# Audio tower, one token layer with attention and a mixture of experts: expert weights split ahead of the first scatter, steps around the expert loop in another order, two groups' expert rows added by accumulating transfers

## The reference

```
h   = gelu(x[1:] @ W1 + x[0] @ W2 + b)                  # per sequence, 255 rows are left
h   = h + attention(layernorm(h))                       # 16 heads of 64, softmax over 255 keys
z   = layernorm(h)
p   = softmax(z @ router_w);  two best experts of 8 per row, with weights p
out = h + sum over the two experts of  p_e * (silu(z @ w1[e]) @ w2[e])
        + sigmoid(z @ gate_w) * ((silu(z @ gate) * (z @ up)) @ shared_down)
```

## Time and profile before

| | us |
|---|---|
| median of three executions | 1126.66 |
| lowest and highest | 1123.14, 1127.31 |
| the profiled execution | 1124.56 |
| its span (first to last recorded work) | 1122.8 |
| TensorE busy | 1054.9 |
| VectorE busy | 767.5 |
| ScalarE busy | 670.2 |
| GpSimd busy | 523.2 |

### The profile page before, as it was taken

The page is one execution under the profiler, slowest core; times in us unless marked ns, Lnnn a source line. Parts: engine busy times, 40 slices in busy tenths (PEclk is TensorE's granted clock), DMA queues, the critical chain, the costliest instruction groups (busy, mean ns, idle before and its releaser), DMA issues.

```text
span 1122.8 us, 23554 instructions
## 1 busy us (share of the span) xinstructions
PE 1054.9 (94%) x8042; PEld 882.3 (79%) x8042; DVE 767.5 (68%) x1975; ACT 670.2 (60%) x2059; POOL 523.2 (47%) x565
## 2 busy tenths in 40 slices
PE   6979999999999999999999999999998968899996
PEld 5867788878777887877788787878767868799985
DVE  3756766785777578577857867775774765466678
ACT  4647775774777477577747757774773534455541
POOL 0024543545546354654635464463444447544432
PEclk9989999999999999999999999999999999899998
DMA  8110000001000000100000010000022723344476
GB/s 262 58 44 1 2 1 20 2 3 38 20 1 30 30 1 1 39 20 1 30 22 9 1 40 20 2 30 16 15 68 84 236 75 112 102 141 134 125 303 212
DMA packets 46442, 65.93 MB, mean 59 GB/s; under 512 B 7960, under 2 KB 39448, under 8 KB 45304
## 3 DMA queue, kind: packets, MB, share of 16 engines
q1 hardware_dynamic: 39576, 46.60, 13.1%
q0 software_dynamic: 6480, 17.83, 4.3%
q10 hardware_dynamic: 272, 0.00, 0.0%
HBM read 36.09 MB, written 28.33 MB: 57 GB/s over the span
## 4 chain that ended last, share of the span: by engine, by line
PE 70%; DVE 9%; POOL 6%; issue 5%; ACT 2%; another core or an unknown queue 1%; DMA 1%; SPq 0%; DVEq 0%; ACTq 0%; POOLq 0%
PE pT_ps L710 10%; PE o_ps L723 9%; PE proj_ps L69 9%; PE proj_ps L71 9%; PE proj_ps L70 8%; PE s_ps L696 8%; POOL prob L1639 3%; PE v_ps L69 2%; POOL prob L1641 2%; PE v_ps L70 2%; PE v_ps L71 2%; PE s_ps L69 2%; PE s_ps L71 2%; PE s_ps L70 2%; PE pT_ps L955 2%
## 5 line engine op out<-in xcount | busy, mean ns | idle before, releaser
L1010 ACT ACTIVATE prob<-s_ps,nmax 128x255 f32<-128x255 f32 x512 | 239.0, 478 | 227.8 <-DVE nmax L1213 227.6
L1639 POOL TENSOR_SCALAR prob<-prob,rinv 128x255 f32<-128x255 f32 x128 | 139.7, 1091 | 373.5 <-DVE rinv L1231 370.6
L1213 DVE TENSOR_REDUCE nmax<-s_ps 128x2 f32<-128x510 f32 x256 | 166.3, 682 | 37.7 <-PE s_ps L696 36.2
L710 PEld LDWEIGHTS pT_ps<-ident,prob 128*128 128x128 f32 x1024 | 109.6, 141 | 60.8 <-issue 49.8
L710 PE MATMUL pT_ps<-ident,prob 128*128 128x128 f32 x1024 | 146.0, 281 | 6.7 <-POOL prob L1641 3.5
L1238 DVE COPY probT<-pT_ps 128x512 f32<-128x512 f32 x128 | 88.5, 691 | 77.0 <-PE pT_ps L710 77.0
L723 PE MATMUL o_ps<-probT,v 128*64 128x256 f32 x1024 | 139.6, 394 | 1.2 <-DVE oT_lo L1244 1.2
L696 PE MATMUL s_ps<-qk_space 64*128 64x256 f32 x1536 | 125.5, 296 | 5.3 <-ACT prob L1010 4.6
L1641 POOL TENSOR_SCALAR prob<-prob,rinv 128x255 f32<-128x255 f32 x128 | 119.2, 931 | 0.0
L696 PEld LDWEIGHTS s_ps<-qk_space 64*128 64x128 f32 x1536 | 99.2, 186 | 21.9 <-issue 8.7
L1010 ACT ACTIVATION_READ_ACCUMULATOR prob<-s_ps,nmax 128x1 f32 x512 | 106.3, 208 | 0.0
(11 more groups left out here) (268 smaller groups left out, 2739.4 us busy)
## 6 DMA issues: line engine op xcount, KB each, us to landing
xg<-expert_in_rows SPq DMA_DIRECT2D x71, 130.0 KB
back<-expert_out_rows SPq DMA_DIRECT2D x8, 1024.0 KB, 13.2
xin<-in_x_dram SPq DMA_DIRECT2D x8, 512.0 KB, 4.5
z_rows<-z SPq DMA_DIRECT2D x8, 512.0 KB, 3.2
z<-z_rows SPq DMA_DIRECT2D x8, 512.0 KB, 5.7
expert_in_rows<-bo_row SPq DMA_DIRECT2D x16, 128.0 KB
raw_up<-in_L_ffn_w_dram SPq DMA_DIRECT2D x8, 256.0 KB, 5.1
raw_down<-in_L_ffn_w_dram SPq DMA_DIRECT2D x8, 256.0 KB, 6.1
```

The costliest lines, as they stand in the source:

```text
L710: m = pe.transpose(pT_ps[h][:, o:o + P], prob[u_par(i)][:, h, qt, kt * P:(kt + 1) * P], ident[:])
L1010: m = act.activation(prob[u_par(i)][:, h, qt, 1:N], s_ps[h][:, qt * N + 1:(qt + 1) * N], ACT.Exp, bias=nmax[u_par(i)][:, n:n + 1], accum_o ...
L1213: dve.tensor_reduce(nmax[u_par(i)][:, 2 * h:2 * h + 2], s_ps[h][:].rearrange("p (q k) -> p q k", q=2)[:, :, 1:N], AX_X, ALU.max, negate=Tr ...
L1639: pool.tensor_scalar(prob[k][:, 0, 1, 1:N], prob[k][:, 0, 1, 1:N], rinv[k][:, 1:2], None, ALU.mult).then_inc(s_nA1, 1)
```

## The change

*Expert weights.* ScalarE makes the high parts of all eight experts ahead of the loop (`split_hi(0)` to `split_hi(7)`, placed between its steps for groups 1 to 3). GpSimd makes all low parts ahead of the first scatter: expert 0 before it waits for the tables, expert 1 behind `hidden_split_lo(2)`, experts 2 to 7 behind `hidden_split_lo(3)`. `split_both` is gone. The order of the weights' loads is the same.

*Ahead of the loop.* `hidden_split_lo` of groups 2 and 3 goes from VectorE to GpSimd. On VectorE `product(2,1)` comes before `z3_lo(3)`, the first two table reductions are a step of their own (`tile_sums`), and `add_shared(3)` comes behind `x_lo(0)` and `x_lo(1)`. On TensorE `shared_rows(3)` comes behind the first two `transpose_x` and `up(0)`.

*End of the loop.* In the last step `transpose_z3(4)` comes before `down_rows(69)`, and `z3_lo(4)` before `y_copy(70)`.

*After the loop.* `hidden_split_lo` of groups 4 to 7 goes from GpSimd to VectorE. The first and second expert rows of all tokens now lie in two halves of `expert_out_rows` (other row numbers in `dest`), and `load_back` takes one piece from each. For groups 0 and 1 nothing is loaded back and VectorE adds nothing: GpSimd issues, behind the last scatter, four transfers that add 512 KB each from DRAM to `resid`; the second of a group waits for its first. `store_group` of these waits for both.

```diff
@@ sync
-            for g in range(2):
+            for g in range(ADDED_BY_DMA, 4):
                 load_back(g)
             load_z3(SHARED_EARLY + 3)
-            for g in range(2, GROUPS):
+            for g in range(4, GROUPS):
                 load_back(g)
...
             def store_group(g):
-                sp.wait_ge(s_all, g + 1)
+                if g < ADDED_BY_DMA:
+                    sp.wait_ge(s_back[g], 16 * TOP)
+                else:
+                    sp.wait_ge(s_all, g + 1 - ADDED_BY_DMA)
@@ tensor
-            shared_rows(SHARED_EARLY - 1)
...
             up(0, e[0])
+            shared_rows(SHARED_EARLY - 1)
             for n in range(RUN):
...
                     transpose_x(n + 2)
+                if n == RUN - 1:
+                    transpose_z3(SHARED_EARLY)
                 if n + 1 < RUN:
                     up(n + 1, e[n + 1])
...
-            transpose_z3(SHARED_EARLY)
             down_rows(RUN - 1, e[RUN - 1])
@@ scalar
             silu(2, 0)
+            split_hi(2)
             z3_hi(3)
             hidden_split_hi(2, 0)
             silu(2, 1)
+            split_hi(3)
             hidden_split_hi(2, 1)
-            split_hi(2)
+            split_hi(4)
+            split_hi(5)
             silu(3, 0)
-            split_hi(3)
+            split_hi(6)
             hidden_split_hi(3, 0)
             silu(3, 1)
+            split_hi(7)
             hidden_split_hi(3, 1)
@@ vector
             product(2, 0)
+            product(2, 1)
             z3_lo(3)
+            tile_sums()
             tile_words()
-            product(2, 1)
-            hidden_split_lo(2)
             add_shared(1)
             product(3, 0)
             product(3, 1)
-            hidden_split_lo(3)
             add_shared(2)
-            add_shared(3)
...
             x_lo(1)
+            add_shared(3)
             for n in range(RUN):
...
+                if n == RUN - 1:
+                    z3_lo(SHARED_EARLY)
             y_copy(RUN - 1)
...
-            z3_lo(4)
             product(4, 0)
             z3_lo(5)
+            hidden_split_lo(4, 0)
             product(4, 1)
-            add_experts(0)
+            hidden_split_lo(4, 1)
             product(5, 0)
+            add_experts(2)
+            hidden_split_lo(5, 0)
             z3_lo(6)
-            add_experts(1)
             product(5, 1)
-            add_experts(2)
+            hidden_split_lo(5, 1)
+            add_experts(3)
+            add_shared(4)
             product(6, 0)
             z3_lo(7)
-            add_shared(4)
-            add_experts(3)
+            hidden_split_lo(6, 0)
             product(6, 1)
             add_experts(4)
+            hidden_split_lo(6, 1)
+            add_shared(5)
             product(7, 0)
-            add_shared(5)
             add_experts(5)
+            hidden_split_lo(7, 0)
             product(7, 1)
+            hidden_split_lo(7, 1)
+            add_shared(6)
             add_experts(6)
-            add_shared(6)
             add_experts(7)
             add_shared(7)
@@ gpsimd
+            split_lo(0)
             pool.wait_ge(s_table, TABLE_STEPS)
-            for e in range(HI_BY_SCALAR):
+            hidden_split_lo(2)
+            split_lo(1)
+            hidden_split_lo(3)
+            for e in range(2, E):
                 split_lo(e)
...
             for n in range(RUN):
                 scatter(n)
-                if n in split_behind:
-                    split_both(split_behind[n])
-            for g in range(SHARED_EARLY, GROUPS):
-                hidden_split_lo(g)
+            def add_experts(g, k):
+                if k:
+                    pool.wait_ge(s_back[g], 16)
+                else:
+                    pool.wait_ge(s_added, 2 * g + 2)
+                rows = y_rows[ROWS * k + GR * g:ROWS * k + GR * (g + 1), :].rearrange("(p t) d -> p (t d)", t=GT)
+                pool.dma_start(resid[:, GT * g:GT * g + GT, :].rearrange("p t d -> p (t d)"), rows,
+                               accum_op=ALU.add).then_inc(s_back[g], 16)
+            for k in range(SLOTS):
+                pool.wait_ge(s_yst[k], 16 * len(range(k, RUN, SLOTS)))
+            for k in range(TOP):
+                for g in range(ADDED_BY_DMA):
+                    add_experts(g, k)
```

More of the change, by code:

```diff
@@ L354, in main_phase @@
     BUFS = 6
-    HI_BY_SCALAR = 4
+    RAW_FIRST = 4
     HEAD = 16
@@ L471, in main_phase @@
         back = [over(f"back{g}", (at["oT_hi"], at["oT_lo"], at["qk_space"], wo_at)[g // 2], g % 2 * GT * TOP * D,
-                     [GT, TOP, D]) for g in range(GROUPS)]
+                     [TOP, GT, D]) for g in range(GROUPS)]
         xgT_hi, xgT_lo = ([over(f"{n}{k}", at["probT1"], (2 * j + k) * DC * P, [DC * P], F32R) for k in range(2)]
@@ L516, in main_phase @@
         s_raw = [sem(f"expert{e}_in") for e in range(E)]
[L517 removed]
+        s_w_hi, s_w = sem("expert_hi"), sem("expert_split")
         s_x_in = [sem(f"xg{k}_in") for k in range(BUFS)]
@@ L527, in main_phase @@
         s_all, s_out = sem("rows_complete"), sem("out_stored")
-        EXPERTS_FIRST = 6
+        EXPERTS_FIRST = 7
+        ADDED_BY_DMA = 2
         FREE_P = 4
@@ L593, in load_back @@
             def load_back(g):
-                sp.dma_start(back[g][:].rearrange("p t k d -> p (t k d)"),
-                             y_rows[TOP * GR * g:TOP * GR * (g + 1), :].rearrange("(p s) d -> p (s d)", s=TOP * GT)
+                sp.dma_start(back[g][:].rearrange("p k t d -> p k (t d)"),
+                             y_rows[0:TOP * ROWS, :].rearrange("(k n p t) d -> p k n (t d)", k=TOP, p=P, t=GT)[:, :, g, :]
                              ).then_inc(s_back[g], 16)
             def store_group(g):
-                sp.wait_ge(s_all, g + 1)
+                if g < ADDED_BY_DMA:
+                    sp.wait_ge(s_back[g], 16 * TOP)
+                else:
+                    sp.wait_ge(s_all, g + 1 - ADDED_BY_DMA)
                 sp.wait_ge(s_added, 2 * g + 2)
@@ L621, in _ @@
             sp.wait_ge(s_wo, 2 * GROUPS)
-            for e in range(HI_BY_SCALAR):
+            for e in range(RAW_FIRST):
                 load_expert(e)
@@ L626, in _ @@
             load_z3(3)
-            for e in range(HI_BY_SCALAR, E):
+            for e in range(RAW_FIRST, E):
                 load_expert(e)
@@ L1403, in z3_lo, with hidden_split_lo @@
                                       ALU.subtract).then_inc(s_zl3, 1)
[L1405 to L1409, removed]
+            def hidden_split_lo(g, c):
+                dve.wait_ge(s_hhi, FC * g + c + 1)
+                dve.tensor_tensor(h_lo[g % 2][:, c, :], h_full[:, c, :], f32(h_hi[g % 2][:, c, :]),
+                                  ALU.subtract).then_inc(s_hlo, 1)
             def product(g, c):
@@ L1418, in add_shared @@
                 if g >= EXPERTS_FIRST:
-                    dve.wait_ge(s_all, g + 1)
+                    dve.wait_ge(s_all, g + 1 - ADDED_BY_DMA)
                 else:
@@ L1522, in _ @@
             dve.wait_ge(s_hlo, FC)
-            hidden_split_lo(1)
+            hidden_split_lo(1, 0)
+            hidden_split_lo(1, 1)
             turns_past()
@@ L1573, in add_experts @@
                     dve.wait_ge(s_woe, 2 * g + 2 + FREE_W)
-                dve.tensor_tensor(rows, rows, back[g][:, :, 1, :], ALU.add).then_inc(s_first, 1)
-                dve.wait_ge(s_first, g + 1)
-                dve.tensor_tensor(rows, rows, back[g][:, :, 0, :], ALU.add).then_inc(s_all, 1)
-            z3_lo(4)
+                dve.tensor_tensor(rows, rows, back[g][:, 1], ALU.add).then_inc(s_first, 1)
+                dve.wait_ge(s_first, g + 1 - ADDED_BY_DMA)
+                dve.tensor_tensor(rows, rows, back[g][:, 0], ALU.add).then_inc(s_all, 1)
             product(4, 0)
             z3_lo(5)
+            hidden_split_lo(4, 0)
             product(4, 1)
-            add_experts(0)
+            hidden_split_lo(4, 1)
             product(5, 0)
+            add_experts(2)
+            hidden_split_lo(5, 0)
             z3_lo(6)
-            add_experts(1)
             product(5, 1)
-            add_experts(2)
+            hidden_split_lo(5, 1)
+            add_experts(3)
+            add_shared(4)
             product(6, 0)
             z3_lo(7)
-            add_shared(4)
-            add_experts(3)
+            hidden_split_lo(6, 0)
             product(6, 1)
             add_experts(4)
+            hidden_split_lo(6, 1)
+            add_shared(5)
             product(7, 0)
-            add_shared(5)
             add_experts(5)
+            hidden_split_lo(7, 0)
             product(7, 1)
+            hidden_split_lo(7, 1)
+            add_shared(6)
             add_experts(6)
-            add_shared(6)
             add_experts(7)
@@ L1702, in split_lo @@
                 m.then_inc(s_w, 1)
[L1704 to L1712, removed]
             router_step(GROUPS, 1)
```

13 lines of the change are left out of this document (6 added, 7 removed).

## The result

The changed kernel takes 1112.9 us (median of 4, 1112.5 to 1114.8), the kernel before 1127.0 on the same chip: 0.9883 of it, 95% interval 0.9861 to 0.9906. The profiled executions have spans of 1111.1 and 1122.8 us: 11.7 us to be found.

What follows compares the result with a forecast made beforehand. TensorE, busy 94% of the span, was taken as the bound, with VectorE in the chain at the end. Terms 3.6 + 6.7 + 0.7 + 3.0 = 14.0 us off 1124.56 give 1110.6, median forecast 1112; eight tenths within 1104 to 1123.

Steps and rivals of the forecast that it cites:

- Term 1: Way into the expert loop: moved splits and new order let transpose_h(0) start at 915.6, 3.6 us earlier.
- Term 2: First 25 tiles of the loop: with the splits gone, most late signals behind back-to-back scatters go, gaining 6.7 us.
- four coincidences: In the loop before: late TensorE signals at 940.10, 948.91, 960.09 and 975.88, each right behind a row of scatters.
- three quarters of the 8.9 us: First 25 tiles: 8.9 us stand in four places with late signals; the change leaves one, so 6.7 us go.
- all of them go: Rival, 12%: in the loop one lag of six scatters costs nothing, 9 to 12.6 us gained, time 1108 to 1106.
- late signals stay: Rival, 17%: late signals in the loop come from instruction count or chance and appear elsewhere; gain 7.3 us, time 1119.
- Term 3: Turn from the loop to the end: transpose_z3(4) and z3_lo(4) one step earlier shorten TensorE's wait, gaining 0.7 us.
- Term 4: After the loop: VectorE does 12 add_experts instead of 16 and takes over eight splits, gaining 3.0 us.
- the 1 us that the prediction worked out from it: End: if adding transfers deliver half of a copy, loads return later and some 1 us is lost: 1113, not 1112.
- stores wait for the adding transfers: Rival, 6%: at the end slow adding transfers hold up the stores; with 27 us a round, time 1138.

Runs made afterwards that it cites:

- e8: The changed kernel with shared_rows(3) and add_shared(3) back ahead of the x transposes, as in the kernel before: 1110.9 us, ratio 0.9866.
- e2: The changed kernel with the weights of experts 4 to 7 again converted and split by GpSimd in the loop, behind scatters 3, 7, 11 and 17: 1119.5 us, ratio 0.9928.
- e5: The changed kernel with eight idle copies on GpSimd behind each of scatters 14, 28 and 42, so late scatters go back to back: 1126.7 us, ratio 1.0008.
- e6: As e5, but a short copy follows the other scatters from 15 on, so late ones go 1.56 us apart: 1112.7 us, ratio 0.9891.
- e10: e2 (splits of experts 4 to 7 in the loop) with one short GpSimd copy behind every scatter: 1113.3 us, ratio 0.9897.
- e7: e1 with hidden_split_lo of groups 4 to 7 on GpSimd again: 1114.3 us, ratio 0.9903.
- e1: The changed kernel with no group's expert rows added by a transfer, two more loads back and four more add_experts: 1115.4 us, ratio 0.9903.
- e4: The changed kernel with the expert rows of four groups instead of two added by transfers: 1116.9 us, ratio 0.9916.
- e9: The changed kernel with one short copy of an idle buffer on GpSimd behind every scatter: 1109.5 us, ratio 0.9866.
- e11: e8 with the copy of e9 behind every scatter: 1110.6 us, ratio 0.9872.
- e3: The changed kernel with TensorE reading the first table word ahead of the first two x transposes instead of behind them: 1112.8 us, ratio 0.9876.

## Why the prediction was right, and where it was not

The median forecast was 1112.0 and the measured one is 1112.9. Behind it one term was too small and two too large: 1.7 + 7.5 + 0.7 + 1.4, and the 0.4 from earlier, are 11.7 us of span in place of 14.0. That the median still came within 1 us is partly luck, since the profiled execution of before lay 2 us under its median and that of the changed kernel did not.

*Term 1, 3.6 us; it was 1.7 (2.1 less the 0.4 that came from earlier).* The early steps held: tables at 901.8, splits at the times given, first scatter at 924.46 (924.5). x was even earlier (909.2 and 910.4, forecast 910.3 and 911.4). What failed is "`up(0)` runs 911.7 to 912.5, `shared_rows(3)` takes 3.1 us (24 matmuls of 0.12)". Behind the short waits TensorE ran at half its clock; 14 matmuls at 0.21 cost 1.3 us. I had priced waits by their length only, and had not seen that the same 24 matmuls took 4.4 us in the kernel before (911.53 to 915.97), 15 of them at 0.21. Beside that stood 0.8 us for reading the table word, which I had not counted. And the step I took for a gain, x transposes ahead of `shared_rows(3)`, was a loss on the way in (`e8`). What gain there is I put down to GpSimd's splits no longer holding up VectorE; the traces fit that, and no run tests it alone.

*Term 2, 6.7 us; it was 7.5, and `e2` gives 6.6 (5.1 by the ratios) for the splits alone.* The mechanism, a cost of scatters back to back, was read from four coincidences and had only 55% with the rest of the forecast; `e5`, `e6` and `e10` show it. Of the first scatters only three came close together, not six, with 0.8 us of waiting on TensorE at 929.76. The size is in part luck. Not three quarters of the 8.9 us went but all of it: tiles 1 to 25 gave 9.2 us, which is "all of them go". Against that tiles 25 to 70 took 1.7 us more (92.6; the other traces but `e5` have 89.9 to 92.1), and no run says why. From first to last `gated` it is 145.7 us, not the 143.5 forecast, because `shared_rows(3)` now runs between the first two (913.76 and 918.53), which the prediction had in term 1 but not in this sign. Two late signals stay, at 928.68 (it cost TensorE the 0.8 us) and at 1026.72, and both stand behind three scatters 1.26 to 1.29 us apart.

The rival "late signals stay" is out. The late signal at 1038.32, which the prediction counted for it, stands behind three scatters back to back too (1033.98 to 1036.52). The Trainium skill, page Runtime: NRT & Kernel Launch, section "Instruction fetch mechanics", has the instruction streams refilled in blocks of 256 instructions, mostly hidden. The traces give no support to late refills as the cause: in the kernel before, the transfer engines carried no instruction packet during the four large waits (938.9 to 940.2, 946.6 to 949.0, 958.2 to 960.1, 973.3 to 975.9), nor in `e5` from 962.8 to 966.1. And in `e10` a copy per scatter adds instructions to GpSimd's stream, and the late signals are gone.

*Term 3, 0.7 us.* The first `product(4,0)` is 7.4 us behind the last `gated`, 8.1 before: 0.7.

*Term 4, 3.0 us.* From that product to the end of the last `add_shared` it is 39.9 us, 42.0 before: 2.1. The last stores then take 0.7 us longer to the end of the span, as the engines are full until 1108 (the earlier trace rows has the last store of before). So the end gave 1.4. The mis-sized part is the cost of adding transfers. A round of two took 11.6 and 8.4 us, forecast 9; 1.8 times the engine time of a copy made the loads back land in 21.2 us at the median (13.2 in the earlier trace rows), and VectorE waited 0.8 us for one at 1088. The Trainium skill, page Collectives: The Full Stack, section "The bandwidth ceiling: the fold count and why AG ≠ RS ≠ AR", says of the reduce step of a collective that its add reads two sources and so delivers half of what a copy does; the trace of these transfers, which are in no collective, nearly agrees (1.7 to 1.8 times a plain one). With the 1 us that the prediction worked out from it the forecast would have been 1113. The 12 `add_experts` took 1.22 us, as forecast. But what pays is not the relief from GpSimd's arithmetic: `e7` against `e1` says that moving the splits is worth nothing by itself. The transfers' gain (`e1`: 2.5 us by the medians, 2.2 by the ratios, 3.0 in the traces) is as much as the end gained or more, though by the times alone it is not settled.

*The rival "stores wait for the adding transfers"* had the right mechanism and the wrong dose: two groups do not reach it, four do (`e4`).

Open: why signals come late behind scatters back to back. The traces show which engines wait and that distance decides, not what carries the signal late. Whether `e8`, `e9` or `e11` is the fastest is not settled; all three lie at 1109.5 to 1111 us with ratios of 0.9866 to 0.9872, below the changed kernel's 0.9883 by less than the intervals.

## What to carry to other kernels

When an engine issues indirect scatters and falls behind, look at what follows the catch-up on the other engines; the remedy can be a copy of 0.4 us between scatters rather than a new plan for the work. A wait that is swapped for several short ones with little work between them need not be cheaper: read the granted clock behind both before choosing the order. Adding transfers relieve VectorE and load the transfer engines by 1.7 to 1.8 times a plain one: here two groups came out ahead in the traces, four did not.

## What the hardware showed that I had not expected

- A scatter 1.27 us behind the last one delays others: three rows of them cost 14 us, 1.56 us apart they cost nothing measurable (`e5`, `e6`), though `e11` has two waits of 0.9 and 1.1 us behind such scatters.
- The profile named GpSimd's split as releaser of `up(0)`; the wait was TensorE's own reading of a word, 0.8 us, found only because `e3` ran ahead of that split.
- An adding transfer takes 1.7 to 1.8 times the engine time of a plain one per MB (`e1`, `e4`).
